# Weighted sums of two steps side by side in one bank, the turned reciprocals in a query fill, the statistics' rows as a fill of their own

## The reference, cut to what matters

```
q = layernorm(x) @ wq + bq ;  k, v = ctx @ wk + bk, ctx @ wv + bv
score = (q k^T / sqrt(32)) * mask ;  score = where(score == 0, -1e9, score)
context = softmax(score) @ v                      # for each head, 128 keys
x = x + context @ wo + bo
x = x + real(ifft(fft(layernorm(x)) @ w)) + b     # 512 -> 512
```

## Time and profile before

| | |
|---|---|
| median of 3 runs | 472.84 us (472.55 to 473.04) |
| profiled execution, its own time | 471.82 us |
| its span | 470.0 us |
| granted TensorE clock, mean | 0.996 |
| busy PE, DVE, ACT, POOL | 449.7, 415.9, 373.9, 364.5 us |

### The profile page before, as it was taken

The page is one execution under the profiler, slowest core; times in us unless marked ns, Lnnn a source line. Parts: engine busy times, 40 slices in busy tenths (PEclk is TensorE's granted clock), DMA queues, the critical chain, the costliest instruction groups (busy, mean ns, idle before and its releaser), DMA issues.

```text
span 470.0 us, 11312 instructions
## 1 busy us (share of the span) xinstructions
PE 449.7 (96%) x3538; PEld 297.8 (63%) x3538; DVE 415.9 (88%) x698; ACT 373.9 (80%) x1431; POOL 364.5 (78%) x519
## 2 busy tenths in 40 slices
PE   6989879898999999999999999999999999999997
PEld 5777557677566666666666666666666666555543
DVE  3797799999999898989999999989898999999552
ACT  3359559789998889899898988898988898899720
POOL 6589657897989979787979797987979882868562
PEclk9999989999999999999999999999999999999999
DMA  8999902332444554444544545353632432341143
GB/s 284 395 352 294 270 11 67 86 86 68 94 105 117 115 135 114 128 120 119 140 108 113 131 102 158 85 137 103 128 78 71 90 82 74 84 91 44 48 112 113
DMA packets 83308, 59.37 MB, mean 126 GB/s; under 512 B 39729, under 2 KB 70705, under 8 KB 82738
## 3 DMA queue, kind: packets, MB, share of 16 engines
q1 hardware_dynamic: 82816, 58.55, 46.2%
q10 hardware_dynamic: 434, 0.10, 0.1%
HBM read 29.27 MB, written 8.39 MB: 80 GB/s over the span
## 4 chain that ended last, share of the span: by engine, by line
PE 80%; DVE 8%; issue 4%; ACT 3%; DMA 2%; POOL 1%; SPq 0%; DVEq 0%; POOLq 0%
PE bank L396 33%; PE bank L468 16%; PE bank L522 10%; PE bank L539 7%; PE bank L401 5%; PE bank L510 5%; PE bank L535 3%; ACT zs L624 2%; DMA cxs<-in_ctx 2%; DVE zs L784 1%; DVE zs L791 1%; PE bank L471 1%; DVE nmin L796 1%; DVE lp L839 1%; POOL x L1002 1%
## 5 line engine op out<-in xcount | busy, mean ns | idle before, releaser
L624 ACT ACTIVATE zs<-zs,nbias 128x128 f32<-128x128 f32 x512 | 199.8, 397 | 19.7 <-POOL nbias L1016 19.6
L624 ACT ACTIVATION_READ_ACCUMULATOR zs<-zs,nbias 128x1 f32 x512 | 99.6, 194 | 0.0
L791 DVE SCALAR_TENSOR_TENSOR zs<-zs 128x1024 f32<-128x1024 f32 x64 | 91.8, 1435 | 2.3
L784 DVE TENSOR_TENSOR zs<-bank,ms 128x512 f32<-128x512 f32 x128 | 82.0, 682 | 0.0
L796 DVE TENSOR_REDUCE nmin<-zs 128x8 f32<-128x1024 f32 x64 | 77.2, 1206 | 0.1
L633 ACT COPY pt<-bank 128x512 f32<-128x512 f32 x128 | 67.8, 582 | 7.0 <-PE bank L522 6.8
L468 PE MATMUL bank<-xth,wqh 128*128 128x256 f16 x256 | 70.7, 276 | 2.2 <-DVE kl L743 1.8
L468 PE MATMUL bank<-xth,wql 128*128 128x256 f16 x256 | 70.2, 274 | 0.0
L468 PE MATMUL bank<-xtl,wqh 128*128 128x256 f16 x256 | 70.1, 274 | 0.0
L522 PE MATMUL bank<-ident,zs 128*128 128x128 f32 x512 | 66.9, 274 | 1.0 <-ACT zs L624 1.0
L522 PEld LDWEIGHTS bank<-ident,zs 128*128 128x128 f32 x512 | 57.4, 140 | 5.7 <-ACT zs L624 4.4
(11 more groups left out here) (109 smaller groups left out, 954.7 us busy)
## 6 DMA issues: line engine op xcount, KB each, us to landing
xs<-in_x SPq DMA_DIRECT2D x16, 512.0 KB, 4.4
xtr<-in_xt SPq DMA_DIRECT2D x16, 512.0 KB, 5.1
out<-x SPq DMA_DIRECT2D x32, 256.0 KB, 2.5
qs<-qh SPq DMA_DIRECT2D x120, 64.0 KB, 2.0
lp<-in_lparts SPq DMA_DIRECT2D x4, 1024.0 KB, 9.8
qs<-ql SPq DMA_DIRECT2D x60, 64.0 KB, 2.0
ms<-in_mask SPq DMA_DIRECT2D x16, 128.0 KB, 2.4
wqs<-in_wq SPq DMA_DIRECT2D x2, 512.0 KB, 6.4
```

Source lines behind the costliest of these rows:

```text
L624: last = act.activation(z, z, ACT.Exp, bias=nbias[:, s % 4, i:i + 1], scale=-NEG, accum_out=zsum[:, s % 4, i:i + 1])
L784: dve.tensor_tensor(zs[:, s % NZ, t], A[n % 2][:].rearrange("p (h k) -> p h k", h=4), ms[:, c % NM, t, :].unsqueeze(1).broadcast_to([128, ...
L791: dve.scalar_tensor_tensor(out=z, in0=z, scalar=0.0, in1=z, op0=ALU.is_equal, op1=ALU.subtract).then_inc(eq_done, 1)
```

## The change

- `weigh` no longer turns the reciprocals. It writes the left half of CX for an even step and the right half for an odd one, and waits for the products of the pair before (`cn_done >= s - s % 2`).
- PV items stand at the start of even slots, ahead of PT, two at a time: steps v-4 and v-3. Before, step v-3 stood in slot v after the scores.
- The two transposes of the reciprocals of step v-3 are issued in slot v at the end of its last late fill (`turn_rz`), into the right half of that fill's bank; `turned` maps a step to this fill. `copy_rec(s)` waits for that fill, and copies from its bank. Where a slot has no late fill (from slot 55), a fill R with the two transposes alone is added.
- The right half of Q(c, 2) being taken, the statistics' rows of chunks 3 to 15 are fills ST of their own, each just ahead of Q(c-1, 2), in slots 3 and 6 and then each slot v with v mod 4 = 1 from 9 to 49.
- `ctx_norm` waits for both sums of its pair; POOL's `spread` waits for the fill that turned the reciprocals two steps before.

```diff
@@ plan()
-        late = [("Q",) + f for f in queries.get(v, [divmod(v + 9, 4)]) if f[0] < NC]
+        late = []
+        for f in queries.get(v, [divmod(v + 9, 4)]):
+            if f[1] == 2 and 3 <= f[0] + 1 < NC:
+                late.append(("ST", f[0] + 1))
+            if f[0] < NC:
+                late.append(("Q",) + f)
+        if 0 <= v - 3 < NS and not late:
+            late.append(("R", v - 3))
...
+        if 0 <= v - 3 < NS:
+            turned[v - 3] = len(fills) - 1
         items = []
+        if v % 2 == 0 and 0 <= v - 4 < NS:
+            items += [("PV", v - 4), ("PV", v - 3)]
         if 0 <= v - 2 < NS:
             items += [("PT", v - 2, 0), ("PT", v - 2, 1)]
         items += [("G", n) for n in mids]
         if 0 <= v + 1 < NS:
             items += [("S", v + 1, 0), ("S", v + 1, 1)]
-        if 0 <= v - 3 < NS:
-            items += [("PV", v - 3)]
         items += [("G", n) for n in lates]
@@ tensor
+            step_of = {n: s for s, n in turned.items()}
+
+            def turn_rz(o, s):
+                pe.wait_ge(p_rz, s + 1)
+                for t in range(2):
+                    last = pe.transpose(o[:, 256 + 128 * t:384 + 128 * t], rzb[:, s % 2, 4 * t:4 * t + 4, :], ident[:])
                 return last
@@ fill
-                    if f == 2 and 3 <= c + 1 < NC:
-                        last = stat_rows(o, c + 1)
...
+                if n in step_of:
+                    last = turn_rz(o, step_of[n])
                 last.then_inc(g_done, 1)
@@ weigh
-                if s >= 1:
-                    pe.wait_ge(cn_done, s)
+                if s >= 2:
+                    pe.wait_ge(cn_done, s - s % 2)
                 else:
                     pe.wait_ge(g_free, at["V", 0] + 1)
-                pe.wait_ge(p_rz, s + 1)
-                for t in range(2):
-                    pe.transpose(CX[:, 256 + 128 * t:384 + 128 * t],
-                                 rzb[:, s % 2, 4 * t:4 * t + 4, :], ident[:])
+                o = slice(256 * (s % 2), 256 * (s % 2) + 256)
                 for j in range(4):
                     h = 32 * (4 * g + j)
-                    last = pe.matmul(CX[32 * j:32 * j + 32, 0:256], vs[:, b, h:h + 32],
+                    last = pe.matmul(CX[32 * j:32 * j + 32, o], vs[:, b, h:h + 32],
                                      pt[:, s % 2, j, :], start=True, stop=True)
@@ scalar
-                    if f == 2 and 3 <= c + 1 < NC:
-                        stat_copy(src, c + 1).then_inc(st_done, 1)
...
             def copy_rec(s):
-                act.wait_ge(pv_done, s + 1)
-                act.copy(rec[:, s % 2, :], CX[:, 256:512]).then_inc(rc_done, 1)
+                act.wait_ge(g_done, turned[s] + 1)
+                if s >= 2:
+                    act.wait_ge(cn_done, s - 1)
+                act.copy(rec[:, s % 2, :], G[turned[s] % 3][:, 256:512]).then_inc(rc_done, 1)
@@ vector
-                elif kind == "ST":
+                elif kind in ("ST", "R"):
...
             def ctx_norm(s):
                 dve.wait_ge(rc_done, s + 1)
+                dve.wait_ge(pv_done, s - s % 2 + 2)
...
-                dve.tensor_tensor(cn[:, s % 2, :], CX[:, 0:256], rec[:, s % 2, :], ALU.mult).then_inc(cn_done, 1)
+                dve.tensor_tensor(cn[:, s % 2, :], CX[:, 256 * (s % 2):256 * (s % 2) + 256], rec[:, s % 2, :], ALU.mult).then_inc(cn_done, 1)
@@ gpsimd, spread
-                    pool.wait_ge(pv_done, s - 1)
+                    pool.wait_ge(g_done, turned[s - 2] + 1)
```

More of the change, by code:

```diff
@@ L34, in plan @@
 def plan():
-    fills, slots, held = [], {}, []
+    fills, slots, held, turned = [], {}, [], {}
     lead = [("W1", 0), ("CT", 0), ("CT", 1), ("K", 0), ("ST", 0), ("Q", 0, 0), ("Q", 0, 1), ("S", 0),
@@ L81, in plan @@
         held = lates
-    return fills, front, slots
+    return fills, front, slots, turned
 def stats_slot(c, t):
@@ L105, in build @@
 def build(nc, x, xt, ctx_in, mask, wq, bq, wk, bk, wv, bv, wo, bo, lparts, tables, bf, eye, sums, pick, out):
-    fills, front, slots = plan()
+    fills, front, slots, turned = plan()
     at = {f: n for n, f in enumerate(fills)}
@@ L408, in stat_rows @@
                 return last
+            step_of = {n: s for s, n in turned.items()}
[3 more added lines that the diff above has]
+                    last = pe.transpose(o[:, 256 + 128 * t:384 + 128 * t], rzb[:, s % 2, 4 * t:4 * t + 4, :], ident[:])
+                return last
             def fill(n):
```

## The result

The changed kernel takes 503.95 us (median of 4 runs, 500.44 to 506.41), the one before 472.69 (4 runs, 472.04 to 473.04): 1.065 times as long, interval 1.062 to 1.0685. The direction was forecast and the size was not: 504 lies above the range of 479 to 499. The profiled execution took 504.79 us, its span 503.0 at a mean granted clock of 0.979; before, 470.0 at 0.996. So 33.0 us of span have to be found.

The account below looks back on a forecast made before the run. PE was taken to bound the kernel's middle, with DVE close behind. Start +6, rounds +11.7 and end -0.5 made +17.2 on the profiled 471.82, 489.0, so 490 as a median; range 479 to 499.

Parts of the forecast that it names:

- PE's own lengths: PE's slot lengths without waits: a pair of sums takes 1.10 in place of 1.34, saving 0.24, 7.7 us over 32 pairs.
- The gate: Reciprocals' copy, first in ACT's slot, waits for PE's previous slot; three-fill slots' query held 1.59, next 0.3; nine rounds +11.7.
- it adds no second delay: In the rounds, DVE is back at the same place after each round, so it adds nothing to the 26.55 us round.
- the hold: In slots with a statistics' fill, PE is held before the query until the previous slot's query is released: 1.59 us.
- The start: Slots 3 to 13, with up to four fills and DVE full: waits add together +6 us, bounds 1 and 10.
- P + 9.9: When DVE's work before its slot 8 ends, counted from PE's start of slot 7; DVE's slot 8 some 4.5 us late.
- the clock's fall: Low clock behind slot 7's wait of 4.4 us: up to 2 us more, left in the range.
- The tail: The end: slots 50 to 54 give back 0.5, from slot 55 pairs buy little; -0.5 us.
- No lost start: Rival: the steady waits come, but the start loses nothing, as idle PE has cover; 485 us, chance 0.17.
- the pair saves nothing: Rival: paired sums save nothing on PE, all slots are 0.12 longer; 495 us, 497 with a clock fall, chance 0.10.
- the gate decides nothing: Rival: the three-fill slot's query bank is released before PE arrives, so the 7.7 us come through; 465 us, chance 0.08.

Follow-up runs that it names:

- e3: Changed kernel with the pair undone: weighted sums one at a time behind the scores again, the rest kept; 502.91 us, ratio 1.063.
- e8: Kernel before plus only the statistics' rows of chunks 3 to 15 as fills of their own; 478.39 us, ratio 1.011.
- e7: Changed kernel with POOL's feed-forward bias addition cut to 8 of 512 columns; 497.49 us, ratio 1.053.
- e6: Changed kernel with one edit: in slot 6 the statistics' fill stands ahead of U(2); 503.05 us, ratio 1.065.
- e9: Changed kernel from step 14 on, steps 0 to 13 as in the kernel before; 490.43 us, ratio 1.039.
- e10: Changed kernel in steps 14 to 51 only, all other steps as in the kernel before; 490.08 us, ratio 1.0375.
- e12: Kernel before with one pair a round in steps 12 to 51, their reciprocals' copy behind ACT's first four exponentials, no third fill; 470.93 us, ratio 0.997.
- e1: Changed kernel without the statistics' fills of chunks 3 to 15, reciprocals turned twice in their place; 477.75 us, ratio 1.010.
- e4: Changed kernel without statistics' fills and with single sums, so only the reciprocals' place and the bank's halves differ from before; 492.58 us, ratio 1.043.
- e2: Changed kernel with ACT's copy of the reciprocals behind its first four exponentials; 491.41 us, ratio 1.036.
- e5: Changed kernel, reciprocals' copy behind ACT's first four exponentials, statistics' fill behind its slot's query, in slot 6 ahead of U(2); 480.95 us, ratio 1.017.

## Why the prediction was wrong in size

**PE's own lengths: right.** The pair takes 1.10 from the slot's start and saves 0.24. The Trainium skill (TensorEngine Tiling, section "Key Properties") says that a change of the tiling mode drains TensorE, and not a change of tile alone; the pair's 16 matmuls within 1.00 us, where one sum takes 0.57, agree. Left out was that PT behind 32-column matmuls takes 0.93 to the next item and not 0.87, twice a round, 0.12.

**The gate: right, to 0.1 us.** rec follows PE's slot start by 0.11 to 0.20 (0.23 forecast), the wait before the query is ended by ql, the slot after it has 0.23. e3 against e8 shows the gate by itself (502.91 and 478.39, rounds of 27.0 and 25.3), and e8 that without it a third fill is nearly free in the rounds. But "it adds no second delay", said of DVE, failed: it is the step that put a term of the rounds at nothing. DVE's starts were right (0.4, 1.4 and 0.7 behind PE and 0.3 ahead), but their meeting with POOL's operations was not looked at. `zero_to_neg` takes 2.32 instead of 1.45 when POOL's bias addition has started first, cn and `least` slip (qh comes 0.15 late, ql another 0.31), and the hold is 2.04 in place of 1.59. A round is 27.01 - 26.55 = 0.46 longer than forecast, nine of them 4.1, and one fall of the clock (the round with the query at 331.83, which took 2.74, is 28.6) adds 1.6: 11.7 + 4.1 + 1.6 = 17.4, and 17.4 is measured. e7 gives 6.5 for the contention as a whole.

**The start: the mis-sized term.** Forecast +6 with bounds 1 and 10, measured 13.4, beyond the upper bound. Slot 7 went as described, up to the wait of 4.25 (P + 9.9 is 9.8 by the terms given, which changes nothing). I had put the clock's fall behind it in the range, "up to 2 us", and not in the sum. It came and cost 3.1 (slot 8 started 7.9 late, 4.8 of which follows from the steps). The Trainium skill (TensorE: Matmul & The Clock Gate, section "Why this matters for your kernels") had asked for no gaps between bursts. The trace agrees for the long wait: the clock is 0.50 behind the 4.25 us, and U(3) is slow in all three traces with that wait (3.57, 3.44 in e3, 3.39 in e7). For shorter waits it is a matter of the single case, as the last section shows. Slot 13 was priced at 0.3, the rounds' value, and had 2.7 us and its own fall, for DVE was already late when it came: PE's lag behind the old times grew by 3.2 in that slot. e6 shows that no single wait of the start can be priced alone.

**The tail: wrong sign.** Forecast -0.5, measured +2.2. DVE reaches the last slots with its mask 0.46 behind PE's PT of slot 54 (415.36 and 414.90), where it was 0.5 ahead of it (383.22 and 383.72). In slots where DVE sets the pace such a lag is not won back. The same meeting with POOL goes on there: `zero_to_neg` takes 17.4 us in slots 53 to 63, 14.8 before. That is 2.6 us on the engine that sets the pace, which fits the loss of 2.2, but no run isolates it. By e9 and e10 the pairs' own waits are worth up to 1.6 us there.

**The rivals.** "No lost start" is refuted by e9, "the pair saves nothing" by the pair's 1.10 us and by e12's rounds, "the gate decides nothing" by e3 against e8. Its half truth is in e1 and e4: I had taken the gate to cost only where three fills meet, and it costs 19 us without them as soon as a sum waits for the product of the step before. That wait is the one that the pair mostly removes.

Sum with measured terms: 13.4 + 17.4 + 2.2 = 33.0. Forecast: 6 + 11.7 - 0.5 = 17.2.

## What to carry to other kernels

Before you move an operand's transposes behind the last item of a slot, look who copies it out and what stands behind that copy in its engine's list; a saving of 0.24 us a pair on PE bought a wait of 0.6 to 2.1 us in each slot of the rounds on ACT. A rotation of three banks bears a third fill in a slot only if the release of the query before comes early, so count for each fill who used its bank last and when that user's release is due. When all engines are as busy as here (78% and more), price a change also by what it shifts against the other engines' long instructions: DVE's and POOL's here took each other's time by who started first. And where a change makes PE wait for some us, put a fall of the clock behind it into the sum, not only into the range; the falls read here cost 1.3 to 3.1 us each. When you compare a round of two kernels, compare the same rounds: those of the kernel before are 25.14 or 25.40, by their place.

## What the runs showed of the hardware

- A DVE instruction of 1024 elements from SBUF to SBUF (`zero_to_neg`) took 1.23 us with its way free. When POOL's addition had started first, it ended 2.34 to 2.37 us after that addition's start, whatever the lead: 2.32 us long for a lead of 0.03 (changed kernel), 2.12 for 0.24 (e4), 1.93 for 0.43 (e3), 1.85 for 0.50 (e9, tail), 1.72 for 0.64 (e2), 1.42 for 0.94 (tails). The addition itself then takes 1.27, so DVE ends 1.08 after the addition does: it looks as if DVE began its work only there. The 1.45 of the kernel before fit this too: they end 1.08 after POOL's `spread`, which ran from 226.87 to 227.27. When DVE had started first, by 0.09 to 0.12 us in e5, it took 1.22 to 1.23, and POOL's addition 2.25 and not 1.27 where DVE was first by 0.34. So who starts first runs at its own length, and the other pays about 1 us. POOL's spans are rough, but this comes out the same in all traces looked at.
- After waits of 2.65, 4.25, 2.56 and 1.88 us PE ran at 1.2 GHz (0.50), for about 6 us after the 4.25. The length of the wait does not decide it alone: the three-fill slots of the rounds have 34 waits of 1.86 to 1.91 us in four traces, and behind four of them the clock fell (1 of 9 in this kernel, 2 of 9 in e6, none of 8 in e9, 1 of 8 in e10), with a round 1.5 to 1.6 us longer each time; and behind a wait of 2.56 us in slot 13 it fell here (the query took 2.75) and not in e6 (1.43). The time of this kernel goes with it: its four runs have 500.44 at a mean clock of 0.989, 503.11 at 0.986, 504.79 at 0.979 and 506.41 at 0.976.
- A change into 32-column matmuls and out of them costs 0.24 us (0.10 ahead, 0.14 behind), whether a query fill or transposes come next, and eight transposes behind it take 0.06 more. A second group of the same shape behind the first costs its own 0.43 alone.
